# DLRM tower with a compressed interaction network: all ten gathers of a tile behind the last pairs of layer 1

## The reference

```
e = stack([tbl_f[ids[:, f]] for f in 39 fields])          # 512 x 39 x 16
prev = e
for k in 0, 1, 2:                                         # 128 units each
    z = einsum('bmd,bhd->bdmh', e, prev)                  # all products of fields with units
    t = transpose(z.reshape(b, 16, m*h) @ w[k] + b[k])
    t = t / sqrt(sum(t*t))                                # norm over units and d, per sample
    logit.append(t); prev = t
f = sum over d of concat(logit)
y = relu(relu([f, dense_ctx] @ W_top1 + b_top1) @ W_top2 + b_top2) @ W_top3
```

## Time and profile before

| what | value |
|---|---|
| time, median of 3 runs | 1181.57 us |
| the runs | 1180.67, 1181.57 and 4874.38 us |
| profiled execution, time | 1181.07 us |
| profiled execution, span | 1179.2 us |
| mean granted TensorE clock, share of full speed | 0.993 |
| PE, DVE, POOL busy, share of span | 95%, 82%, 74% |
| gathers (L243) | 160, together 155.4 us, 971 ns each |
| L278 and L281 on POOL | 192 each, 1277 and 2372 ns |

### The profile page before, as it was taken

The page is one execution under the profiler, slowest core; times in us unless marked ns, Lnnn a source line. Parts: engine busy times, 40 slices in busy tenths (PEclk is TensorE's granted clock), DMA queues, the critical chain, the costliest instruction groups (busy, mean ns, idle before and its releaser), DMA issues. The chain is left out here.

```text
span 1179.2 us, 21810 instructions
## 1 busy us (share of the span) xinstructions
PE 1124.8 (95%) x7868; PEld 568.1 (48%) x7868; DVE 972.1 (82%) x836; ACT 126.4 (11%) x266; POOL 868.3 (74%) x614
## 2 busy tenths in 40 slices
PE   0789999999999999999999999999999999999999
PEld 0344445455444545544454554545455454545553
DVE  1678889889898988988898898989889898988782
ACT  0000110101011010101101011110101011010102
POOL 5567768788786878877686886868788786856670
PEclk9889999999999999999999999999999999999999
DMA  5958446382744638274463837546382845637010
GB/s 163 382 150 277 142 165 211 98 294 68 286 131 162 210 96 299 68 280 136 144 220 97 306 68 263 154 167 208 95 296 68 282 134 176 211 104 274 1 47 1
DMA packets 104409, 204.31 MB, mean 173 GB/s; under 512 B 49131, under 2 KB 52075, under 8 KB 104390
## 3 DMA queue, kind: packets, MB, share of 16 engines
q1 hardware_dynamic: 97610, 202.52, 51.9%
q0 software_dynamic: 5120, 1.29, 1.1%
q10 hardware_dynamic: 1660, 0.25, 0.2%
HBM read 201.72 MB, written 2.30 MB: 173 GB/s over the span
## 5 line engine op out<-in xcount | busy, mean ns | idle before, releaser
L560 DVE TENSOR_TENSOR z<-t_ps,xb 128x2048 f32<-128x2048 f32 (+1 forms) x352 | 708.1, 2042 | 97.6 <-PE acc L711 73.8
L281 POOL TENSOR_TENSOR sums<-z,sums 128x1024 f32<-128x1024 f32 x192 | 455.4, 2372 | 15.1
L697 PE MATMUL acc<-z,w_sb 128*64 128x512 f32 x1920 | 436.5, 598 | 12.5 <-DVE z L560 12.5
L278 POOL TENSOR_TENSOR sums<-z 128x512 f32<-128x512 f32 x192 | 245.2, 1277 | 193.0 <-DVE z L560 189.2
L711 PE MATMUL mix_ps<-sums,s_sb 128*64 128x256 f32 x1536 | 282.6, 380 | 6.0 <-POOL sums L281 6.0
L697 PEld LDWEIGHTS acc<-z,w_sb 128*64 128x64 f32 x1920 | 137.8, 138 | 246.8 <-issue 224.8
L711 PE MATMUL acc<-z,w_sb 128*64 128x256 f32 x768 | 228.4, 379 | 0.0
L711 PE MATMUL mix_ps<-z,w_sb 128*64 128x256 f32 x768 | 228.4, 379 | 0.0
L711 PE MATMUL acc<-z,s_sb 128*64 128x256 f32 x768 | 228.4, 379 | 0.0
L711 PE MATMUL p_ps<-z,w_sb 128*64 128x256 f32 x768 | 228.4, 379 | 0.0
L711 PEld LDWEIGHTS mix_ps<-sums,s_sb 128*64 128x64 f32 x1536 | 158.8, 137 | 93.6 <-POOL sums L281 13.1
(11 more groups left out here) (76 smaller groups left out, 404.9 us busy)
## 6 DMA issues: line engine op xcount, KB each, us to landing
xb<-xt SPq DMA_DIRECT2D x80, 768.0 KB, 6.8
xb<-xq SPq DMA_DIRECT2D x96, 512.0 KB, 4.7
xb<-xt SPq DMA_DIRECT2D x96, 512.0 KB, 6.3
xr<-xt SPq DMA_DIRECT2D x144, 156.0 KB
x<-xt SPq DMA_DIRECT2D x45, 78.0 KB
gathered<-in_table,rows_of POOLq DMA_INDIRECT x160
xr<-xt SPq DMA_DIRECT2D x32, 78.0 KB
xt<-gathered SPq DMA_DIRECT2D x16, 72.0 KB, 2.3
```

What stands on the lines that cost most here:

```text
L278: nc.gpsimd.tensor_tensor(t2, t3, b11, ALU.add).then_inc(sums_ready, 1)
L281: nc.gpsimd.tensor_tensor(t41, b2, t2_twice, ALU.subtract).then_inc(sums_ready, 1)
L560: nc.vector.tensor_tensor(z[:, at:at + n, :], t_ps[k - 1][:, :].rearrange("p (a n) -> p a n", a=1).broadcast_to([P, n, N]), xb[:, XB_ROW[c ...
L697: last = nc.tensor.matmul(acc[k][o, :], w_sb[k][:, field + r, o], z[:, at + r, :], start=(c == 0 and r == 0), stop=(c == NCH - 1 and r == ...
```

## The change

The call of `gather` behind the last pair chunk of layer 1 issues all ten groups instead of the first five; the call behind the last pair chunk of layer 2 goes. `gather` itself and its waits are as before, and so are SP's and PE's programs.

```
                         if k == 1 and c == LAST_P and gathers:
-                            gather(i + 2, range(0, 5))
-                        if k == 2 and c == LAST_P and gathers:
-                            gather(i + 2, range(5, GROUPS))
+                            gather(i + 2, range(GROUPS))
```

## The result

The changed kernel took **1195.54 us** (median of four runs, 1194.52 to 1197.63), the kernel before beside it 1181.12: a ratio of 1.0126 [1.0106, 1.0146], slower by 1.3%, under the 2% that counts as a difference here. (One of the four runs of the kernel before took 4874 us and is left out of the ratio.) The forecast was 1186.5 in a range of 1178 to 1194: the sign was right, the size was a third of what came, and the time lies 1.5 us above the range. The profiled execution took 1195.27 us, its span is 1193.4 us for 1179.2, at a mean granted clock of 0.991 for 0.993. Code lines after the change have numbers two lower: L558 is DVE's product `z`, L695 `direct`, L709 `pairs`, L686 `layer0`.

The account below looks back on a forecast made before the run. PE, busy for 95% of the span, was taken as the bound, standing still where POOL's gathers delay its sums. -7.7 + 2.2 + 10.7 = +5.2 us on 1181.07 gave 1186.3, 1186.5 as median; range 1178 to 1194.

Parts of the forecast that it names:

- The pauses: Behind layer 1: five POOL pauses, one in 29 gathers, no longer covered and passed whole to PE; 10.7 us in all.
- my upper bound: Pauses among the ten gathers behind layer 1: all five at 3.31 us, 15.1 us in all.
- slack of 1.02 us: Layer 1 to layer 2: POOL's tight sum may end 1.02 us later, at 588.26 for 587.24, without costing PE.
- The overhang: Ten gathers behind layer 1 make POOL's sum 1.18 us late, 0.16 us beyond PE's slack; 2.2 us over 14 tiles.
- dearer overhang: Rival: 0.34 us gap ahead of the sum and 3.31 us pauses behind layer 1; +14.1, 1195 us; chance 0.15.
- The gain behind layer 2: Five gathers removed there: 0.08 us in 11 ordinary tiles plus 6.85 us for three pauses, 7.7 us in all.
- all shift together, since PE has nothing to catch up with: First layer-2 pair chunk: POOL's sums behind the gathers, PE and DVE's later products move together; costed at nothing.
- I cost both at nothing: Queue effects on POOL (layer-2 sums behind gathers) and SP (gathered rows' write behind field loads): no cost.
- a new wait of DVE for x or xr rows: Sign that the forecast is wrong: DVE newly waiting for those rows; no size given.
- Harmless pauses: Rival: pauses depend on time between groups, or a block of gathers leaves the memory empty; 1175.6 us; chance 0.13.
- Slow gathers: Rival: two of the five moved gathers slowed beside other work, 27 us more, 1213 us; chance 0.04.
- No net effect: Rival: gains and losses equal by no overhang in ordinary tiles and shorter pauses; 1181 to 1183 us; chance 0.08.

Follow-up runs that it names:

- experiment 4: Changed kernel with dynamic_dma_scratch_size 2048 for 4096, half the room for POOL's descriptors: 1205.91 us, 1.02.
- Experiment 1: Changed kernel with SP's loads of the next tile's xb held until the product that frees chunk 4's place: 1190.32 us, 1.0068.
- experiment 9: Changed kernel with one more semaphore and eight increments of it at the start of POOL's program, which nothing waits for: 1193.18 us, 1.0105.
- experiment 2: Kernel before with seven gathers behind layer 1 and three behind layer 2, for five and five: 1176.97 us, 0.9962.
- Experiment 14: Changed kernel with SP's xb loads held back and one more semaphore with eight idle increments at POOL's start: 1187.4 us, 1.005.
- 13: Changed kernel run once more, unedited: 1196.18 us in a single profiled run.
- 3: Kernel before with five additions of 448 columns on POOL behind its five gathers of layer 1: 1182.42 us, 1.0006.
- 6: Kernel before with nine gathers behind layer 1 and one behind layer 2: 1184.93 us, 1.0028.
- 10: Changed kernel with one more semaphore and eight idle increments of it at the start of ACT's (ScalarE's) program: 1193.32 us in a single profiled run.
- 11: Changed kernel with one more semaphore that nothing uses, no instruction more: 1196.54 us in a single profiled run.
- 12: Changed kernel with eight increments at POOL's start on the existing semaphore rows_seen, no semaphore more: 1199.85 us in a single profiled run.
- 7: Changed kernel with POOL waiting ahead of the sixth gather until the first five have landed: 1224.17 us in a single profiled run.
- 8: Changed kernel with two POOL additions between the fifth and sixth gather, no wait: 1223.04 us in a single profiled run.
- eight and two: Kernel before with eight gathers behind layer 1 and two behind layer 2: 1176.27 us, 0.9957.
- experiment 15: Kernel before with eight gathers behind layer 1, two behind layer 2, and dynamic_dma_scratch_size 6144 for 4096: 1174.41 us, 0.994.

## Why the forecast was right in kind and too small in size

The sum of the forecast was +5.2 us, the span grew by 14.2. Its steps, against the trace after:

**The pauses.** That they come back, in which tiles and at which gather, and that each passes whole to PE, was right; experiment 4 shows that their count goes with the size of the descriptor memory (one gather in 14 with 2048, one in 29 with 4096). The step that failed is "I take 2.24 for the 5th, 6th and 7th, 2.5 for the 8th, 3.0 for the 9th": they were 2.28, 2.23, 2.76, 3.98 and 4.60. The 8th and 9th are above my upper bound too, the longest pause of the trace before, 3.31. The five together are 3.6 us longer than assumed. The windows showed the DMA engines full from 578 us on; I used them to choose between 2.24 and 3.31 instead of asking how long the last gathers issued into that traffic would take to land. Experiment 1, with the loads held, gives 2.20 to 2.40. That a delay of POOL passes whole to PE beyond its slack of 1.02 us holds: in tile 6 the sum is 3.64 us late and the tile 2.61 us longer.

**The clock**, not in the forecast: in tiles 0 and 3 PE stood and its clock fell to 0.50 for about 3 us (what lowers it, no run tests); what those tiles take beyond the pause and the overhang, 0.7 + 1.0 = 1.7 us, I put down to that.

**The overhang.** 0.16 us per tile was right: 0.19 in experiment 9, where nothing else disturbs it. The sum started within 0.01 us of the forecast. The rival *dearer overhang* gave 1195 us, nearest to the result, and that is luck: its gap of 0.34 us ahead of the sum is 0.02, so its 6.7 us are 2.7; its pauses came near in their sum (15.1 us for 14.4 measured) but not one by one; and it knew neither the clock nor the hold.

**The gain behind layer 2.** The 0.08 us per tile was false (experiment 2), 0.9 us of the 7.7. The other 6.85, the three pauses that go, were there: those tiles took 2.00, 1.89 and 2.68 us over 68.26 before, 6.6 in all.

**The hold and PE's late second stream**: a second step that failed, "all shift together, since PE has nothing to catch up with", and "I cost both at nothing". Ordinary tiles take up to 0.72 us over 68.26 instead of 0.19. Over the eight measured distances that is 4.55 - 8 x 0.19 = 3.0 us. The ninth has no successor; from its first gather to the end it is 201.45 us, and 201.49 in experiment 9, without the hold, so it adds nothing that shows. I had named a new wait of DVE for x or xr rows as a sign of being wrong; the new wait, 1.27 us, is for PE.

**The account.** 5.2 + 3.6 (pauses) + 1.7 (clock) + 3.0 (PE's late second stream) + 0.9 (no gain) + 14 x 0.03 (overhang) + 0.3 (6.6 for 6.85) = 15.1; the first gather of tile 0 comes at 83.14 for 84.34 us, 1.2 earlier, so 13.9 against 14.2 measured. That start differs from run to run (82.56 to 85.28 us over all traces here), so I take the 1.2 us for chance. Experiment 14, without the longer pauses and without the late second stream, comes back to 1187.4, within 1 us of the forecast, and 6.3 us above the kernel before beside it where the forecast has 5.2: that the two together are the bulk of the miss is shown. The share of each is read off the traces, and 14 does not separate them.

**The other rivals.** *Harmless pauses* fell by the five pauses. *Slow gathers* fell: gathers beside products of `t_ps` and `xb` stay at 0.92 to 0.95 us, and the one of 1.89 us lay beside a product of two SBUF operands. So did one of 1.91 us in the same trace (it starts at 31.90, the product at 31.77) and one of 2.00 us in the trace after (28.87 and 28.83). What slows them is not shown. *No net effect* fell too: it wanted no overhang and shorter pauses, and the overhang is 0.19 us and the pauses are longer.

**What stays open** is why the engines go on late. Shown: it is a property of the program and not of the run (13); it isn't the loads (1), a busy POOL (3) or the number of gathers as such (6, 9, 10); in the changed kernel itself a pause at the 5th, 6th or 7th gather removes it (squares at 9.6 in tiles 12, 9 and 6) and one at the 8th or 9th shortens it (10.2 and 11.4 in tiles 3 and 0); it goes with a semaphore and eight increments at the start of POOL or of ACT, stays with either half alone (11, 12), and is back with both once the loads are late (14). That points to where the program's parts lie rather than to what the tiles do, but this is argued, not shown, and no run tells late signals from engines that are late to act on them. Why PE's second stream starts late with the hold in one program and not in another (14) is open too. That 7 and 8 removed the hold by breaking the ten fits what a pause does, but their added semaphore and shifted programs were not tested apart from it.

## What to carry to other kernels

The indirect DMAs here have a cost that comes by count: at one in 29 of them (one in 14 or 43 with another `dynamic_dma_scratch_size`) POOL stands, by the signs of experiments 4 and 7 until the earlier ones have landed. So look in the trace for a pause that comes by count, move groups such that it falls into spare time (here eight and two, 5 us) and try more room (6144 for 4096, 1.4 us more). Price such a pause by what the DMA queues carry at its new place (up to 4.60 us beside loads, 2.20 to 2.40 us with them held back), not by the shortest one seen at the old. Part of a small miss (here 3 of 9 us) can hang on the program and not on the work in it: a variant that differs only in idle instructions shows that.

## What the runs showed of the hardware

- POOL's pause came once in 14, 29 and 43 gathers with `dynamic_dma_scratch_size` at 2048, 4096 and 6144 (experiment 4; the kernels before and after; experiment 15). It was 2.17 to 2.40 us with the loads held back (experiments 1 and 14) and in tile 0 up to 6.12 and 6.23 us beside loads (experiments 9 and 8; 312 and 303 GB/s in the windows from 93 to 95 and 95 to 97 us, in the pause of 9).
- TensorE's granted clock fell to 0.50 after waits of 2.23 and 1.77 us close together (tile 0 after) and of 0.93 and 1.77 us (tile 3), and stayed at 1.00 where PE waited once for 1.75 us (tile 6). It was at 0.50 for about 3 us both times, and for 6 us in tile 0 of experiment 9, where PE waited 3.77 and 1.30 us and the fall began in the first of the two (0.93 from 101 to 102 us, 0.50 from 102).
- ACT went on 4.8 us late (14.4 for 9.6 us) behind a signal of PE in each ordinary tile of some programs and not of others with the same instructions in the tiles; DVE then waited 1.15 to 1.47 us where it had not waited.
- A POOL sum that came 1.85, 3.64 or 1.17 us late cost the tile 0.84, 2.61 or 0.19 us (experiment 3, tile 12; the changed kernel, tile 6; experiment 9): the lateness less about 1.0 us.
